# Value products of two heads in one 32-column strip: one and two heads per strip in three attentions of a one-core kernel

## The reference

```
q = (Q @ Wq.T).reshape(B, S, H, Dk).transpose(0, 2, 1, 3)
k = (K @ Wk.T).reshape(B, S, H, Dk).transpose(0, 2, 1, 3)
v = (V @ Wv.T).reshape(B, S, H, Dk).transpose(0, 2, 1, 3)
scores = jnp.einsum('bhqd,bhkd->bhqk', q, k) / jnp.sqrt(jnp.float32(Dk))
attn = jax.nn.softmax(scores, axis=-1)
ctx = jnp.einsum('bhqk,bhkd->bhqd', attn, v)
return ctx.transpose(0, 2, 1, 3).reshape(B, S, E) @ Wo.T
```

## Time and profile before

| what | us |
|---|---|
| median of three runs | 1466.67 (1466.66 to 1469.27) |
| profiled execution, span | 1467.0 |
| PE busy | 1171.7 (80%) |
| DVE busy | 988.9 (67%) |
| ACT busy | 667.1 (45%) |
| POOL busy | 538.9 (37%) |

### The profile page before, as it was taken

How to read it: one execution, slowest core, us unless ns; L and a number is a source line. 1 busy time by engine, 2 the same in 40 slices (tenths; PEclk the granted TensorE clock), 3 DMA queues, 4 the chain that set the end, 5 groups by cost and what they waited for, 6 DMA issues and landing times. The chain is left out here.

```text
span 1467.0 us, 34935 instructions
## 1 busy us (share of the span) xinstructions
PE 1171.7 (80%) x11141; PEld 918.1 (63%) x11154; DVE 988.9 (67%) x2920; ACT 667.1 (45%) x1423; POOL 538.9 (37%) x590
## 2 busy tenths in 40 slices
PE   2699994439999957779987879999799956499991
PEld 1477773338899925556673456677477755399991
DVE  3689996474443347998984679888477777766552
ACT  1367762105555503345564546766234343144440
POOL 2324201664235256534411232431121125752554
PEclk9999997559999967899998989999799988599996
DMA  6887743012223258435532177564200042133542
GB/s 179 206 215 191 188 124 129 29 33 87 77 92 109 75 133 209 122 101 144 150 84 51 44 176 167 150 163 106 86 1 0 0 152 74 53 120 106 149 140 73
DMA packets 138978, 164.58 MB, mean 112 GB/s; under 512 B 15308, under 2 KB 118754, under 8 KB 131728
## 3 DMA queue, kind: packets, MB, share of 16 engines
q1 hardware_dynamic: 130664, 146.62, 37.0%
q0 software_dynamic: 8192, 16.46, 4.1%
HBM read 111.98 MB, written 51.38 MB: 111 GB/s over the span
## 5 line engine op out<-in xcount | busy, mean ns | idle before, releaser
L586 DVE TENSOR_REDUCE A_neg_max<-A_s_bank 128x4 f32<-128x512 f32 x384 | 253.2, 688 | 46.3 <-PE A_s_bank L725 35.9
L448 ACT ACTIVATE A_probsT<-A_st_bank 128x512 f32<-128x512 f32 x384 | 222.4, 602 | 40.4 <-PE A_st_bank L738 39.2
L725 PE MATMUL A_s_bank<-A_k_stack,A_q_stack 72*128 72x128 bf16 x1536 | 157.5, 228 | 38.0 <-DVE A_neg_max L586 22.3
L738 PE MATMUL A_st_bank<-A_q_stack,A_k_stack 128*128 128x128 bf16 x1536 | 153.1, 224 | 7.1 <-DVE A_q_stack L602 6.2
L738 PEld LDWEIGHTS A_st_bank<-A_q_stack,A_k_stack 128*128 128x128 bf16 x1536 | 112.5, 103 | 52.2 <-issue 42.9
L725 PEld LDWEIGHTS A_s_bank<-A_k_stack,A_q_stack 72*128 72x128 bf16 x1536 | 106.3, 102 | 52.1 <-DVE A_neg_max L586 33.4
L752 PE MATMUL A_pv_bank<-A_probsT,A_v_pad 128*32 128x128 f32 x3072 | 127.4, 284 | 1.5 <-issue 1.5
L2041 ACT ACTIVATE E_h<-E_h_bank,w_L_b 128x256 f32<-128x256 f32 x184 | 76.8, 471 | 72.4 <-PE E_h_bank L2141 71.0
L2153 PE MATMUL E_y_bank<-E_w,E_h 128*128 x736 | 90.3, 276 | 2.2 <-ACT E_h L2041 0.9
L752 PEld LDWEIGHTS A_pv_bank<-A_probsT,A_v_pad 128*32 128x32 f32 x3072 | 74.1, 111 | 24.7 <-issue 3.4
L2141 PE MATMUL E_h_bank<-E_xT,E_w_u 128*128 128x256 f32 x368 | 88.8, 386 | 0.0
(11 more groups left out here) (371 smaller groups left out, 2641.4 us busy)
## 6 DMA issues: line engine op xcount, KB each, us to landing
A_q_stack<-q_scratch SPq DMA_DIRECT2D x48, 576.0 KB
A_k_stack<-k_scratch SPq DMA_DIRECT2D x32, 576.0 KB
q_scratch<-A_q_parts SPq DMA_DIRECT2D x48, 192.0 KB, 2.3
A_k_stack<-k_scratch SPq DMA_DIRECT2D x48, 192.0 KB
E_xe<-slots_in SPq DMA_DIRECT2D x53, 128.0 KB, 2.1
slots_out<-E_ye SPq DMA_DIRECT2D x53, 128.0 KB, 1.7
A_ctxT<-in_ctxT SPq DMA_DIRECT2D x24, 256.0 KB, 10.5
k_scratch<-A_k_parts SPq DMA_DIRECT2D x32, 192.0 KB
```

What stands on the lines that cost most here:

```text
L448: act.activation(probsT[n % 2][:, c * HQ:(c + 1) * HQ, :], st_bank[c % 2][:, :].rearrange("k (a q) -> k a q", a=HQ), ACT.Exp, scale=scale) ...
L586: dve.tensor_reduce(neg_max[:, c * HQ:(c + 1) * HQ], s_bank[c % 2][:, :].rearrange("q (a k) -> q a k", a=HQ), AX.X, ALU.max, negate=True). ...
L725: last = pe.matmul(s_bank[c % 2][:, a * S:(a + 1) * S], q_stack[slot][0:COMBO, h, at:at + S], k_stack[slot][0:COMBO, h, at:at + S], start= ...
L738: last = pe.matmul(dst, k_stack[slot][:, h, at:at + S], q_stack[slot][:, h, at:at + S], start=True, stop=spread)
```

## The change

Two heads share a 32-column strip. Each piece of `v_pad` gets nine columns of zeros ahead of the first head (`PAIR` = 9). For an even head the stationary operand starts at the head's values, as before; for the odd head of the pair it starts nine columns earlier, so its 8 values and its column of ones stand in columns 9 to 17 and the columns ahead are zeros. The even head's matmul begins a sum in the strip and the odd head's adds to it. Eight heads fill one 128-column piece, so an entry's result is 128x256: `outT` and the copy into it shrink to 256 columns, and PE makes two transposes in place of four. `divide` reads the values and sums at steps of 9 and 32. `probs_v` is called twice in an entry with eight heads each, and waits for both quarters' exponentials before its first matmul.

```diff
-        v_pad = [sb(f"v_pad{i}", [S, GB, vheads, VW], F32) for i in range(2)]
+        v_pad = [sb(f"v_pad{i}", [S, GB, PAIR + vheads * VW], F32) for i in range(2)]
...
-                act.copy(outT[:, :, :].rearrange("p a q -> p (a q)"), pv_bank[:, :]).then_inc(ot_copied, 1)
+                act.copy(outT[:, :, :].rearrange("p a q -> p (a q)"), pv_bank[:, 0:2 * S]).then_inc(ot_copied, 1)
...
-                out = t_bank[:, :].rearrange("q (c a v) -> q c a v", a=HQ, c=4)
-                sums = rsum[:, :].rearrange("q (c a) -> q c a", c=4)
+                out = t_bank[:, 0:2 * S].rearrange("q (s v) -> q s v", v=VW)[:, :, 0:2 * PAIR].rearrange(
+                    "q s (o v) -> q s o v", v=PAIR)
+                sums = rsum[:, :].rearrange("q (s o) -> q s o", o=2)
...
-            def probs_v(b, n, c):
-
-                pe.wait_ge(exp_done, 4 * b + c + 1 + CREDIT)
-                if c == 0:
+            def probs_v(b, n, half):
+
+                pe.wait_ge(exp_done, 4 * b + 2 * half + 2 + CREDIT)
+                if half == 0:
                     pe.wait_ge(ot_copied, b + 1)
                 p = n // GB % 2
-                for a in range(HQ):
-                    h = c * HQ + a
-                    last = pe.matmul(pv_bank[a * VW:(a + 1) * VW, c * S:(c + 1) * S],
-                                     v_pad[p][:, n % GB, h % vheads, :], probsT[n % 2][:, h, :], start=True, stop=True)
-                if c == 3:
+                for odd in range(2):
+                    for a in range(STRIPS):
+                        h = 2 * (half * STRIPS + a) + odd
+                        begin = PAIR + (h % vheads) * VW - odd * PAIR
+                        last = pe.matmul(pv_bank[a * VW:(a + 1) * VW, half * S:(half + 1) * S],
+                                         v_pad[p][:, n % GB, begin:begin + VW], probsT[n % 2][:, h, :],
+                                         start=(odd == 0), stop=(odd == 1))
+                if half == 1:
                     last.then_inc(pv_done, 1)
...
-                for a in range(HQ):
+                for a in range(2):
                     last = pe.transpose(t_bank[:, a * S:(a + 1) * S], outT[:, a, :], core.ident[:, :])
```

More of the change, by code:

```diff
@@ L91, in multi_head_attention @@
     kd = DH if shared_kv else D
+    PAIR = DH + 1
+    NS = NH // 2
+    STRIPS = NS // 2
     vheads = 1 if shared_kv else NH
@@ L156, in multi_head_attention @@
         hi, lo = MAX_ROWS.start, MAX_ROWS.start + (NH if spread else 32)
-        outT = sb("outT", [128, HQ, S], F32)
+        outT = sb("outT", [128, 2, S], F32)
         rsum = sb("rsum", [S, NH], F32)
@@ L326, in values @@
             src = prep_bank[:, :].rearrange("k (b h d) -> k b h d", b=GB, h=NH)[:, :, 0:vheads, :]
-            dst = v_pad[p][:, :, :, 0:DH]
+            dst = v_pad[p][:, :, PAIR:].rearrange("k b (h v) -> k b h v", v=VW)[:, :, :, 0:DH]
             if shared_kv:
@@ L347, in fill @@
                 for t in v_pad:
-                    own.did(pool.memset(t[:, :, :, :], 0.0))
+                    own.did(pool.memset(t[:, :, :], 0.0))
                 own.wait()
                 for t in v_pad:
-                    pool.memset(t[:, :, :, DH:DH + 1], 1.0).then_inc(fill_done, 1)
+                    pool.memset(t[:, :, PAIR:].rearrange("k b (h v) -> k b h v", v=VW)[:, :, :, DH:DH + 1], 1.0)\
+                        .then_inc(fill_done, 1)
             def late_rows(begin, end):
@@ L608, in divide @@
                 dve.wait_ge(t1_ready, START + b)
-                out = t_bank[:, :].rearrange("q (c a v) -> q c a v", a=HQ, c=4)
-                sums = rsum[:, :].rearrange("q (c a) -> q c a", c=4)
+                out = t_bank[:, 0:2 * S].rearrange("q (s v) -> q s v", v=VW)[:, :, 0:2 * PAIR].rearrange(
+                    "q s (o v) -> q s o v", v=PAIR)
+                sums = rsum[:, :].rearrange("q (s o) -> q s o", o=2)
                 own.link(dve.reciprocal(sums, out[:, :, :, DH]))
-                dve.tensor_tensor(out_n[:, :].rearrange("q (c a d) -> q c a d", c=4, a=HQ), out[:, :, :, 0:DH],
-                                  sums[:, :, :, None].to_broadcast([S, 4, HQ, DH]), ALU.mult).then_inc(o_norm, 1)
+                dve.tensor_tensor(out_n[:, :].rearrange("q (s o d) -> q s o d", s=NS, o=2), out[:, :, :, 0:DH],
+                                  sums[:, :, :, None].to_broadcast([S, NS, 2, DH]), ALU.mult).then_inc(o_norm, 1)
             def add_x(b, n=0):
@@ L850, in entries @@
                     probs_v(b, n, 0)
-                    probs_v(b, n, 1)
                     transpose_out(b)
@@ L856, in entries @@
                     project_out(b)
-                    probs_v(b, n, 2)
-                    probs_v(b, n, 3)
+                    probs_v(b, n, 1)
             with pe.Fori(0, last_round) as it:
```

## The result

The changed kernel takes 1462.10 us (median of 14 runs), the kernel before, run beside it, 1470.61 us (14 runs). The ratio is 0.9937, with an interval from 0.9920 to 0.9954: 0.63% or some 9 us less (6.8 to 11.8), where 8.6 us were forecast. It is this difference that was met: the forecast of 1458 us was taken from three runs of the kernel before (1466.67), which beside the changed kernel ran 3.9 us longer, and 1462.10 us lies 0.1 above the stretch that the prediction thought likeliest (1455 to 1462), inside its range (1450 to 1466). A second comparison, beside the last experiments, gave 0.9922 [0.9896, 0.9948]. The profiled execution of the changed kernel took 1461.49 us, with a span of 1459.6 us.

What follows compares the result with a forecast made beforehand. The prediction took the loop between PE and DVE as the bound. Plain entries 2.2, groups 4.4, second attention 0.4 and tails 1.6 summed to 8.6 us off 1467.0: 1458 us, likeliest 1455 to 1462, range 1450 to 1466.

Steps and rivals of the forecast that it cites:

- The plain entry: Entries without projection work: +0.14 − 0.08 − 0.22 = −0.16 us each, −2.2 us over 14, inside the 0.19 DVE can give.
- The wait: Second half of the value product waits for the fourth exponential before its first matmul: +0.14 us a plain entry.
- The two transposes: Last two of four `outT` transposes on PE go, on the loop with DVE: −0.22 us an entry.
- The copy: ACT's `pv_bank` copy, 512 to 256 columns: 0.21 us shorter, of which 0.08 us comes back in a plain entry.
- Rival 2: Value product's wait costs what the transposes save, 0.30 instead of 0.14 in a plain entry: about −1 us, 1466; chance 0.16.
- The groups of the first attention: Four entries with projection work, DVE waiting for PE in two: −0.44 us a group, five groups.
- The groups of the third attention: Same −0.44 us a group as in the first attention, five groups; advance kept in the next two entries.
- Rival 4: Q projection entry: the shift parts DVE's L594 from POOL's L312, 10 × 0.4 us more gain: 1454; chance 0.04.
- The tails: Each attention's last two entries and drain: −0.11 us twice and −0.33 in the drain, −1.6 us over three.
- rival 5: Less PE work lets its clock fall, priced on the 14 plain entries: 22 us more, 1480; chance 0.02.
- Of the rivals, 1: Everything DVE loses to PE comes back, in plain entries, groups and tails: 15.6 us, 1451; chance 0.14.
- rival 3: Value product's strips lose pace through unaligned loads or adding odd heads, a half growing by 0.47 us: 1504; chance 0.06.

Runs made afterwards that it cites:

- e4: Kernel before, with both quarters of a half of the value product waiting for the later exponential: 1479.76 us, ratio 1.0055.
- e2: Changed kernel with the copy of `outT` 512 columns wide again, still two transposes: 1468.27 us, ratio 0.9973.
- e1: Changed kernel with four transposes again, two into columns nobody reads; 256-column copy and wait by halves stay: 1473.60 us, ratio 1.0008.
- e5: Changed kernel with GpSimd's output bias addition in the third attention cut to 2 of 128 columns: 1459.08 us, run once.
- e6: Kernel before with GpSimd's output bias addition in the third attention cut to 2 of 128 columns: 1472.08 us, run once.
- e3: Changed kernel with strips pairing heads of two quarters, so each pass waits only for its own exponential: 1460.98 us, ratio 0.9908.
- after_again: The changed kernel, unaltered, run once more beside the last experiments: 1461.74 us.

## Why the prediction was right, step by step

**The plain entry.** Forecast −0.16, measured −0.19, all that DVE had to give. The wait is +0.14 (e4), as priced. The two transposes are −0.22 (e4 to e2), as priced. The copy was mis-sized: −0.08 was forecast, e4 to e1 shows −0.14. The step that failed took the copy's end and PE's own readiness and counted the 0.08 between them. Missed was that transposes behind a wait also take longer, 0.49 us against 0.44: where PE comes late, their first weight load starts 0.05 us ahead of the first product (203.33 and 203.38 in e1), behind the wait the two start together (204.64 and 204.65 in e2; 206.51 both in the kernel before). 0.08 + 0.05 is the 0.14 within the reading. The three terms make −0.22, and DVE's own 4.47 us cuts that to −0.19. Rival 2, a bare load behind the wait for the exponential that eats the gain, is out: it needed 0.30, and e4 shows 0.14.

**The groups of the first attention.** Forecast −0.44, measured −0.50, from the same three terms twice: e4 adds 0.17 (forecast 0.16), the copy takes off 0.23 to 0.28 (forecast 0.16), the transposes 0.39 to 0.44 (forecast 0.44). L625 (L620 before) comes 0.23 us earlier in the group, as forecast, and still waits 0.18 us for PE (0.24 before), since DVE too is earlier. That is the group from the ninth entry on; the next three gained 0.50, 0.28 and 0.77, and why they differ was not taken apart. In the profile after, DVE's waits in that group (total, times, longest) have no line for the maxima left, which were 0.3 there before:

```profile
DVE x_sb L625 <- PE A_wo_bank L788: 0.2, 1, 0.2
DVE A_mv L548 <- DVE A_stats L544: 0.2, 1, 0.2
```

**The groups of the third attention.** Forecast −0.44, measured −0.27 to −0.29 in three groups, −0.08 in the one before them and −0.78 in the one behind them, where no addition meets the normalising. DVE's waits did fall; in the group from 922.82 to 945.38 the line of the earlier trace rows is gone and what is left of waits for PE is

```profile
DVE x_sb L625 <- PE A_wo_bank L788: 0.4, 1, 0.4
```

The sentence that failed is that the advance "is kept, since nothing in the next two entries waits for PE". It is not a wait that took it. Counted from the group's start, DVE came to the normalising 0.56 us earlier and GpSimd's addition only 0.28 earlier; DVE met more of the addition, and the pair took longer by what DVE had come closer. Rival 4 had this mechanism, with another instruction and the hope of a gain; L598 (L594 before), which it named, takes 0.57 us in both kernels. e5 and e6 show the cause: without the addition the two attentions gain alike, 0.56 and 0.50.

The Trainium skill, "SBUF — State Buffer", section "Who interferes with whom", calls the port pair that VectorE and GpSimd share an exclusive lock. The overlaps of the last section agree that DVE doesn't get past the addition, but not that it gets nothing done beside it: if the first normalising could only begin at the addition's end, the pair would end 0.60 us behind it, and it ends 0.34 behind it. The row that the prediction took for agreement says the same: L594, which takes 0.17 us alone, ends 0.02 behind L312 and not 0.17.

**The second attention.** Forecast −0.4 for four groups; its groups from the 13th, 17th and 21st copy into `q_stack` went from 24.59, 25.69 and 24.61 to 24.73, 25.40 and 24.61 us. The middle one gains 0.29, and the same 25.69 and 25.40 stand in e6 and e5, whose code for this attention is that of the two kernels; the last gains nothing, and the first differs as much between executions of one kernel (24.59 and 24.83 in e6). That little was at stake was right.

**The tails.** Forecast −1.6 in the three, measured about −0.3. From the start of the attention's 29th copy into `q_stack` to that of the last addition of a product it is 22.09 us before and 21.59 after, and 0.38 of that are its two plain entries. The tail entries themselves grew, the first from 3.89 to 3.97, the second from 3.85 to 3.97. ACT and PE in a tail before:

```profile
220.34 1.09 ACT L448 ACTIVATE A_probsT<-A_st_bank 128x512 f32<-128x512 f32 x2
...
221.36 0.65 PE L752 MATMUL A_pv_bank<-A_probsT,A_v_pad 128*32 128x128 f32 x16
...
222.53 0.60 ACT L448 ACTIVATE A_probsT<-A_st_bank 128x512 f32<-128x512 f32 x1
...
223.04 0.64 PE L752 MATMUL A_pv_bank<-A_probsT,A_v_pad 128*32 128x128 f32 x16
```

and after:

```profile
216.85 1.09 ACT L452 ACTIVATE A_probsT<-A_st_bank 128x512 f32<-128x512 f32 x2
...
217.99 0.38 PEld L759 LDWEIGHTS A_pv_bank<-A_probsT,A_v_pad 128*32 128x32 f32 x16 [0.26 <-ACT A_probsT L452]
...
219.16 0.60 ACT L452 ACTIVATE A_probsT<-A_st_bank 128x512 f32<-128x512 f32 x1
...
219.81 0.64 PE L759 MATMUL A_pv_bank<-A_probsT,A_v_pad 128*32 128x128 f32 x16
```

The first half began 0.07 us ahead of the end of the second exponential (221.43) before, and begins 0.05 behind it now (217.94): +0.12. The second half went from 0.09 ahead to 0.05 behind: +0.14. In e4 the two waits cost 0.26 in this entry, and from e2 to the changed kernel the copy gives 0.18 back: +0.08, the measured change. The step that failed is "the first half waits for the second exponential, done well before it is reached; no cost". That holds in a plain entry, where scores stand between, and not in the tail, where ACT is what PE waits for. The prediction's −0.11 doesn't follow from its own terms either: −0.21 + 0.14 is −0.07. The drain, from the last copy into `outT` to the last addition of a product, gained more than forecast: 3.18 us before and 2.75 after, −0.43 (0.21 + 0.22, the copy and two transposes) for −0.33. e3, where each pass waits for its own exponential, shows the tail that the prediction had in mind and more: 3.67 us, 0.22 less than before.

One drain of the changed kernel shows what rival 5 feared. That of the second attention takes 3.20 us, and in its second half the granted clock (third from the end of the row) is 0.50, the lower level, 1.2 GHz:

```profile
777.00:778.88 1.88, 1.19 (x3) 0.60 (x3) 0.29 (x1) 0.27 (x1) 0.00 (x0) 0.50 0.00 0
```

In the 1.60 us before that PE was busy for 0.51. Of nine drains in three executions of the changed kernel's code (after, after_again, e5) seven take 2.75 us, this one 3.20 and another, in e5, 3.05; the three of the kernel before take 3.18 at 1.00. So the price is up to 0.45 us in a drain.

**The sum.** From the start of an attention's ninth copy into `q_stack` to that of its last addition of a product, the first attention lost 3.37 us (129.59 to 126.22) and the third 2.52 (131.24 to 128.73); the prediction's terms for these stretches come to 3.1 each (five plain entries, four groups, a tail). Both repeat to 0.02 us in after_again. Together they are 5.9 of the some 9 us measured.

The rest is not located. The two profiled executions differ by 7.4 us; outside those two stretches that is −4.3 ahead of the ninth copy in the third attention, −0.2 there in the first, +2.0 in the second attention and +1.0 outside the three. But these parts scatter: the second attention took 217.4 us in the kernel before and 223.1 in e6, which has the same code there, and the stretch ahead of the ninth copy in the third took 47.15 and 48.62 in two executions of the changed kernel. One part looks like a loss: in the second attention, between the 27th and the 28th copy, PE waits for a transfer into `q_stack` 2.8 us before and 3.1 in e6, but 4.6 in the changed kernel, 4.8 in after_again and 5.3 in e5. Why is not shown. For all that is not located the prediction had 2.4 us, which the scatter neither shows nor excludes.

So the total was met with errors that partly cancel: the copy and the drains were worth more than forecast, the tail entries and the third attention less. That 8.6 comes so close is in part luck. Of the rivals, 1 holds for the plain entries alone; the price of rival 3 counts 15 groups where the prediction elsewhere has 14.

## What to carry to other kernels

When one wait for several producers replaces a wait for each, price it at every place where the code runs: where the producer is the bound, it costs its full lead each time, and regrouping the data so that each pass needs one producer wins it back (0.30 us a tail entry here). When an engine gets ahead, look not only at who it waits for next but at what runs on GpSimd beside its next instructions; moving GpSimd's step to a stretch where nobody meets it gave 0.48 us a group here.

## What the runs showed of the hardware

DVE's normalising beside GpSimd's addition ends at a fixed time, whenever it starts. (Spans on GpSimd are rough, but what follows repeats to 0.01 us.) From the addition's start to DVE's, then the length of the pair: 0.89 and 0.72 us before, 0.83 and 0.78 in e1, 0.61 and 0.99 after, 0.53 and 1.08 in e3. Each sum is 1.60 or 1.61, which is the addition's 1.27 and 0.34 more, somewhat over half of the undisturbed pair's 0.60. In the other groups and in e2, e4 and after_again it is the same: 35 overlaps that start 0.17 to 0.97 us into the addition, and the pair always ends 0.34 or 0.35 behind it. The one of e3:

```profile
921.12 1.27 POOL L379 TENSOR_TENSOR x_sb<-x_sb,w_L_bo 128x512 f32<-128x512 f32 x1 [0.27 <-POOL A_q_parts L317]
...
921.65 1.08 DVE L560 TENSOR_SCALAR A_xn<-x_sb,A_mv,A_rstd 128x128 f32 x2
```

It isn't the tensor that both touch that does this. The last addition of the third attention meets DVE's copy into `q_stack`, which has no tensor in common with it and takes 0.69 us alone; after the change:

```profile
987.75 1.27 POOL L379 TENSOR_TENSOR x_sb<-x_sb,w_L_bo 128x512 f32<-128x512 f32 x1 [0.27 <-POOL A_q_parts L317]
...
988.42 1.15 DVE L606 COPY A_q_stack<-A_max_rows 32x2048 bf16<-32x2048 bf16 x1
```

It ends 0.55 behind the addition; before, where it started later and took 0.88, also 0.55. What is left behind GpSimd's end is fixed for an instruction and larger for the one that moves more: 0.02 us for the cast of 16 columns (L594, 0.17 alone), 0.08 for a normalising of 128 (0.35 alone), 0.55 for the copy of 2048. So 0.14 to 0.27 us of each isn't held up; that this is its start, and the rest its pass over the data, fits the numbers and is not shown.

A run of transposes that begins behind a wait takes 0.05 us more than one that PE reaches late: 0.49 against 0.44 for four, 0.27 against 0.22 for two.
